# Second attention of a two-layer attention and mixture-of-experts kernel: order of context and X loads, shared root steps, and earlier routing steps

## The reference, cut to what matters

```
B, S, D, KEYS, E = 16, 112, 256, 375, 8
x = x + xattn0(layernorm(x), ctx)          # 16 heads, projections
x = x + ffn0(layernorm(x))                 # top-2 of 8 experts, gelu, per-expert capacity
# second layer: what the change touches
q = layernorm(x)
e = (q @ ctx.T) / sqrt(D)                  # per batch, 112 x 375
e = e - (1 - mask[b, s]) * 1e9
x = x + softmax(e) @ ctx                   # per batch, 112 x 256
# second ffn
logits = layernorm(x) @ gate_w             # 112 x 8 per batch
mult, sel = sparse_mixer(logits)           # top 2 of 8, two gates per token
x = x + sum over chosen experts of w * (silu(x w1) * (x w3)) w2
```

## Time and profile before

| | |
|---|---|
| median of three runs | 1080.9 us (1079.68 to 1085.33) |
| the profiled execution: its time, its span | 1085.0 us, 1083.1 us |
| PE, DVE, ACT, POOL busy | 949.7, 685.8, 544.7, 478.4 us |
| mean granted clock of PE | 0.937 |
| DMA | 160.1 MB, mean 148 GB/s |
| last layer-0 row in PSUM read by DVE; first hidden matmul of layer 1 | 615.29 us; 755.64 us |

### The profile page before, as it was taken

One profiled execution on the slowest core, in us unless ns is written; L12 is line 12 of the kernel. 1 busy time (PEld: TensorE's weight loads), 2 busy tenths in 40 slices (PEclk: granted clock), 3 DMA queues, 4 the chain that ended last, 5 costly groups with the idle time before them and its releaser, 6 DMA issues.

```text
span 1083.1 us, 23135 instructions
## 1 busy us (share of the span) xinstructions
PE 949.7 (88%) x8011; PEld 872.0 (81%) x8011; DVE 685.8 (63%) x1937; ACT 544.7 (50%) x1212; POOL 478.4 (44%) x478
## 2 busy tenths in 40 slices
PE   4889999999999568999999758772999999999997
PEld 4778888778877468998999735562999999999997
DVE  6456676676666666666666435674667788777242
ACT  3678888878888545455555313321323433433120
POOL 2022235225223346666666523376355455545323
PEclk9799999999999779999999969875999999999999
DMA  7878888977774268667766685544353445433101
GB/s 187 166 211 186 201 196 214 247 182 188 188 169 108 60 184 209 152 160 160 182 165 163 150 208 163 163 134 151 118 141 93 106 113 153 113 100 81 20 3 23
DMA packets 109671, 160.10 MB, mean 148 GB/s; under 512 B 11361, under 2 KB 98625, under 8 KB 107617
## 3 DMA queue, kind: packets, MB, share of 16 engines
q1 hardware_dynamic: 95600, 140.03, 49.3%
q0 software_dynamic: 13936, 18.33, 8.7%
HBM read 103.32 MB, written 56.96 MB: 148 GB/s over the span
## 4 chain that ended last, share of the span: by engine, by line
PE 43%; DVE 8%; POOL 5%; issue 4%; DMA 4%; ACT 1%; POOLq 0%; SPq 0%; DVEq 0%; ACTq 0%
PE ps L300 37%; DVE HTH L1293 2%; POOL x_scratch L1545 2%; PE ps L647 1%; PE ps L490 1%; DMA CN<-in_ctx_n 1%; PE ps L578 1%; POOL xg_scratch L1481 1%; DMA x_scratch<-YY,XG 1%; POOL rs L1460 1%; DVE WL L915 1%; PE ps L595 1%; POOL HTL L1533 1%; DVE st L1113 1%; DMA XG<-xg_scratch 1%
## 5 line engine op out<-in xcount | busy, mean ns | idle before, releaser
L300 PE MATMUL ps<-XGH,WH 128*128 128x280 f32 (+1 forms) x768 | 224.9, 293 | 9.6 <-ACT GT L816 7.4
L300 PE MATMUL ps<-XGL,WH 128*128 128x280 f32 (+1 forms) x768 | 224.1, 292 | 0.0
L300 PE MATMUL ps<-XGH,WL 128*128 128x280 f32 (+1 forms) x768 | 223.9, 292 | 0.0
L1533 POOL TENSOR_TENSOR HTL<-GT,HTH 128x280 fp32r<-128x280 f32 x128 | 132.6, 1049 | 168.3 <-DVE HTH L1293 168.3
L1165 DVE CUSTOM_DVE_ANT_0 NS<-ps,negm 112x375 f32<-112x375 f32 x256 | 138.0, 545 | 91.2 <-PE ps L406 90.1
L300 PE MATMUL ps<-WH,HTH 128*112 128x256 f32 x568 | 162.1, 285 | 1.5 <-DVE YY L1307 1.5
L300 PEld LDWEIGHTS ps<-XGH,WH 128*128 128x128 f32 x768 | 148.9, 194 | 14.4 <-ACT GT L816 10.8
L300 PE MATMUL ps<-WL,HTH 128*112 128x256 f32 x568 | 159.6, 281 | 0.0
L300 PE MATMUL ps<-WH,HTL 128*112 128x256 f32 x568 | 159.5, 281 | 0.0
L744 ACT ACTIVATE PP<-NS,MN 112x375 f32<-112x375 f32 x256 | 156.8, 613 | 3.4 <-DVE MN L1165 2.9
L300 PEld LDWEIGHTS ps<-XGH,WL 128*128 128x128 f32 x768 | 149.1, 194 | 0.0
(11 more groups left out here) (206 smaller groups left out, 1893.4 us busy)
## 6 DMA issues: line engine op xcount, KB each, us to landing
WG<-in_v SPq DMA_DIRECT2D x48, 512.0 KB, 4.1
KST<-k_scratch SPq DMA_DIRECT2D x48, 376.0 KB, 5.5
WG<-in_w SPq DMA_DIRECT2D x32, 512.0 KB, 4.5
k_scratch<-KHL SPq DMA_DIRECT2D x64, 188.0 KB
CT<-in_ctx_t SPq DMA_DIRECT2D x32, 375.0 KB, 7.4
xg_scratch<-zero SPq DMA_DIRECT2D x8, 1289.8 KB, 10.3
xg_scratch<-zero SPq DMA_DIRECT2D x16, 586.2 KB, 9.0
XG<-xg_scratch SPq DMA_DIRECT2D x14, 586.2 KB, 4.6
```

The costliest lines, as they stand in the source:

```text
L300: m = e.matmul(out_ap, l, r, start=n == 0, stop=n == len(steps) - 1)
L1533: e.tensor_tensor(HTL[:, f, cols], GT[:, gi % 3, :], HTH[:, f, cols], ALU.subtract).then_inc(hl_pool[layer], 1)
```

## The change

- `CHUNKS1` becomes 3, 3, 3, 3, 2, 2.
- CT2 and CN are moved in memory behind the tile XG of layer 0, over the tiles that the hidden and the row matmuls read, so they can be loaded once those matmuls are done.
- In the last expert of layer 0, ACT, DVE and POOL handle chunks 38 and 39 before the row blocks (DVE: chunk 38 before the first).
- SP issues CT2(0) and CT2(1) before the last two weight chunks (after the last hidden matmul), CN(0) after the last row matmul, and only then waits for the row adds. After them: X 0 to 1, X 2 to 3, CT2(2), CN(1), X 4 to 7, CT2(3), CN(2), X 8 to 15, CN(3), then CT2(4) and so on, CT2(b) with CN(b-4) from b = 8.
- POOL waits for both statistics of a step and does both roots with one addition and one power.
- DVE's stage order becomes `attended`, `inverse`, `mins`, `normed4`, `normed3`, `stats3`; up to three routing instructions are placed behind each and six at the end of a step, the older group first. A group's lists begin at the end of step 11, counts and exponential come in step 13, DVE's part behind them right after `attended` of that step (after `normed4` in the last step).
- POOL's scatter of batch b comes at step 12 + nb + b while the step is below 23, the rest after the last root.

```
+                last = layer == 0 and ex == E - 1          # ACT, POOL; DVE alike, inside the row loop
+                for c in range(per - 2 if last else 0):
+                    lo(base + per * ex + 10 + c)
...
+            for t in range(B + 9):
+                for stage, fn in ((8, attended), (6, inverse), (4, mins), (9, normed4), (1, normed3), (0, stats3)):
                     if 0 <= t - stage < B:
                         fn(t - stage)
+                        if stage == (8 if t < B + 8 else 9) and t >= 13:
+                            counted(t - 13)
+                        advance_pairs(routes, 3)
+                if t >= 11:
+                    route(t - 11)
+                advance_pairs(routes, 6 if t < B else 12)
...
+            def roots(t):
+                new, old = t - 1 < B, t - 9 >= 0
+                if new:
+                    e.wait_ge(var3, t)
+                if old:
+                    e.wait_ge(var4, t - 8)
+                i = (t - 1) % 2
+                cols = slice(4 + i if new else 6 + i, 7 + i if old else 5 + i, 2)
+                if t > 2:
+                    e.wait_ge(rs34, t - 2)
+                e.tensor_scalar(rs[:, cols], st2[:, cols, 1], EPS, None, ALU.add).then_inc(eps, 1)
...
+                e.tensor_tensor(rs[:, cols], rs[:, cols], half, ALU.pow).then_inc(rs34, 1)
...
+            for t in range(1, B + 9):
+                roots(t)
                 for b0, nb in CHUNKS1:
+                    if 0 <= t - 12 - b0 - nb < nb and t < B + 7:
+                        pool_scatter(e, 1, sent)
+                        sent += 1
+            for b in range(sent, B):
+                pool_scatter(e, 1, b)
...
+                if layer == 0 and ex == E - 1:
+                    e.wait_ge(h_mm[0], 16 * E)
+                    context_t(e, 0)
+                    context_t(e, 1)
...
+            e.wait_ge(y_mm[0], 5 * E)
+            context_n(0)
+            for n in range(5 * E - NY, 5 * E):
+                e.wait_ge(*row_done(0, n))
             kept(0)
+            kept(1)
+            context_t(e, 2)
+            context_n(1)
+            kept(2)
+            context_t(e, 3)
+            context_n(2)
+            kept(3)
+            context_n(3)
+            for b in range(4, B + 4):
+                if b < B:
+                    context_t(e, b)
+                if b - 4 >= 4:
+                    context_n(b - 4)
```

More of the change, by code:

```diff
@@ L846, in act_experts @@
                     n = base + per * ex + 10 + c
-                    if c < per - 2 and n < NCHUNK:
+                    if c < per - 2 and n < NCHUNK and not last:
                         act_weights_hi(e, n)
@@ L890, in gate_exp, with gate_after @@
                 e.activation(v, v, ACT.Exp, scale=-1.0).then_inc(r_exp, 1)
[L892 to L895, removed]
+            def gate_after(b):
+                if ends_chunk1(b) is not None:
+                    gate_exp(ends_chunk1(b))
+            for t in range(B + 13):
+                for stage, fn in ((11, logits_out), (13, gate_after), (10, x4_out), (6, copies), (5, exps), (2, x3_out)):
                     if 0 <= t - stage < B:
@@ L1084, in build_kernel, with __init__, step @@
         class Route:
-            def __init__(self, steps):
-                self.steps, self.at = steps, 0
+            def __init__(self, steps, order=(0, 0)):
+                self.steps, self.at, self.order = steps, 0, order
+            def step(self, routes):
+                Chain.at = self.at
+                got = next(self.steps, "end")
+                self.at, Chain.at = Chain.at, Chain.n
+                if got == "end":
+                    routes.remove(self)
+                return got not in ("end", "blocked")
         placed = set()
@@ L1095, in advance @@
                 for r in list(routes):
[L1096 to L1101, removed]
+                    if r.step(routes):
                         if in_turn:
@@ L1105, in advance, with advance_pairs @@
                         break
+        def advance_pairs(routes, n):
+            taken = 0
+            for i in range(n):
+                for r in sorted(routes, key=lambda r: (r.order[0], (r.order[1] + i) % 2)):
+                    if r.step(routes):
+                        taken += 1
+                        break
+            return taken
         def dve_flags(e, layer):
@@ L1327, in dve_experts @@
                             lo(n)
+                last = layer == 0 and ex == E - 1
                 for c in range(5):
@@ L1561, in pool_experts @@
                             lo(n)
+                last = layer == 0 and ex == E - 1
+                for c in range(per - 2 if last else 0):
+                    lo(base + per * ex + 10 + c)
                 for c in range(5):
                     rows_added(ex, c)
-                    if c < per - 2:
+                    if c < per - 2 and not last:
                         lo(base + per * ex + 10 + c)
@@ L1785, in sp_attention1 @@
         def sp_attention1(e):
-            for n in range(5 * E - NY, 5 * E):
-                e.wait_ge(*row_done(0, n))
             def kept(i):
```

100 lines of the change are left out of this document (51 added, 49 removed).

## The result

The changed kernel takes 1078.97 us (median of 20 runs, 1069.23 to 1087.74), the kernel before 1083.03 beside it on the same chip (20 runs, 1077.05 to 1090.71). The ratio is 0.9957, with an interval of 0.9936 to 0.9977: 4 us faster, just inside the 0.5% that one measurement can tell. The forecast was 1069.7 and its range ended at 1076, so both are missed. It started from a median of 1080.9 for the kernel before, which over 20 runs is 1083.03; so 2.1 us of the miss are the base, and the rest is the gain, 4 us for 11.2. What came is near the size of rival C: only the tail gains.

What follows compares the result with a forecast made beforehand. Second attention was taken as bound by a hole, a 4.70 us loop, routing and a scatter tail, with CN's DMA engines close behind. Gains 5.4 + 0.8 + 5.0 = 11.2 us from 1080.9 gave 1069.7, range 1059 to 1076.

Steps and rivals of the forecast that it cites:

- rival C: Second attention: early loads only displace X, the queue decides, only the tail gains 5 us: 1076; chance 0.13.
- 5: DMA engines carrying CN: CN(15) lands at 710.5 to 711; batch 15 taken as attended at 714, 5.4 us sooner.
- step 3: Start of second attention: no wait for CN(0), batch 0 6.3 us sooner; PE then stands 5 to 6 us for CT2(4).
- the third: The 5 of 16 DMA engines said to carry each 125-partition CN load, 3.26 us apiece, and never to rest.
- Step 1: Chunks 38 and 39 before the rows: the last row add goes at about 617.0, a gain of 0.5 us.
- Step 2: Early CT2(0), CT2(1) and CN(0) fill the queue: X 0 to 1 lands at about 627, a loss of 3 us.
- Step 4: Attention loop, shared root and new DVE order: steps of 3.6 to 4.4 us, plus 3.4, put batch 15 at 714.5.
- Step 6: Routing counts at step 13, bank freed behind `attended`: PE's 3.71 us stand and the slow matmuls after it go.
- Step 7: Tail: 16 scatters behind the last root instead of 20, 5.0 us less; the last root follows batch 15 0.8 sooner.
- B: Second attention: DMA has room and the loop runs at PE's pace, batch 15 at 704: 1059.7; chance 0.20.
- D: POOL in order: shared root held behind scatters waiting for destinations, up to 3 us a step, slower: 1090.3; chance 0.07.
- A: The forecast itself: 5 us of the gain in the stage, 6 behind it, range 1064 to 1074; chance 0.60.

Runs made afterwards that it cites:

- the scatter run: Changed kernel with the scatters placed three steps later, 20 behind the last root instead of 16; ratio 0.9996 to the kernel before.
- second and third group: Follow-up runs, against the kernel before at 1109.1 and 1110.7 us; every profile shows a lower granted clock, 0.915 to 0.928.
- first and fourth group: Follow-up runs, against the kernel before at 1082.3 and 1082.5 us; granted clock 0.936 to 0.940 and 0.928 to 0.943.

## Why the prediction was wrong

**The step that failed is 5**, with 3, which it was to confirm: "CN(15) lands at 710.5 to 711, so batch 15 is attended at 712 to 713", because the third "never rests" and starts with two CT2 and one CN done. It did rest, and PE's wait for CT2(4), put at 5 to 6 us in step 3, was 8.78 and 9.60. Windows of 2 us (busy PE, PEld, DVE, ACT, POOL, clock, DMA share, GB/s), and SP's issues:

```profile
650.00:652.00 2.00, 0.00 (x0) 0.00 (x0) 0.00 (x0) 0.00 (x0) 0.00 (x0) 0.50 0.47 131
652.00:654.00 2.00, 1.77 (x3) 1.07 (x4) 0.00 (x0) 0.00 (x0) 0.00 (x0) 0.50 0.32 116
654.00:656.00 2.00, 2.00 (x6) 1.22 (x5) 0.92 (x4) 0.36 (x1) 0.00 (x0) 0.50 0.05 19
```

```profile
634.87 4.14 SPq L1866 DMA_DIRECT2D CN<-in_ctx_n  x1
639.05 16.39 SPq L1808 DMA_DIRECT2D CT<-in_ctx_t  x5
655.49 0.38 SPq L1866 DMA_DIRECT2D CN<-in_ctx_n  x1
659.05 0.38 SPq L1808 DMA_DIRECT2D CT<-in_ctx_t  x1
659.47 0.36 SPq L1866 DMA_DIRECT2D CN<-in_ctx_n  x1
```

Four buffers hold CT2. CT2(8) can be issued only when `scores` of batch 4 have run, and those stood 8.78 us for CT2(4). CN(4) is behind CT2(8) in SP's order, so it goes at 655.49, into engines whose share has fallen to 0.05. Most of the head start of 7 us of loads is used up at that moment. My own arithmetic with the right start gives: eight pairs at 4.6, four CN at 3.26 and three stores at 2.3 are 56.7, from 655.5 that is 712.2, against 713.5 in the kernel before. The value matmuls of batches 12, 13 and 14 wait, and batch 15's follow at 713.81; with the CN load cut these waits are gone, so it is CN that they wait for:

```profile
701.52 1.52 PE L597 MATMUL ps<-CN,PT 125*112 125x256 f32 x6 [1.25 <-issue]
...
704.98 1.52 PE L597 MATMUL ps<-CN,PT 125*112 125x256 f32 x6 [1.07 <-issue]
...
710.12 1.66 PE L597 MATMUL ps<-CN,PT 125*112 125x256 f32 x6 [1.70 <-issue]
```

Batch 15 is attended at 717.25 for the 714 forecast. Of these 3.25 us the later start explains about 1.5 (712.2 for 710.5 to 711). The rest is argued and not shown: batch 15's value matmuls begin 1.6 us behind that sum and run at a granted clock of 0.50. In the second profile batch 15 is at 119.8 instead of 116.5 behind the last hidden matmul, for which I have no cause. Point by point:

- **Step 1**, last row add at 617.0, gain 0.5: wrong, 620.18, a loss of 2.7. I looked at ACT's gate and not at the buffer of the row copy. The row add issued at 609.54 took 8.81 us, and the fifth copy needs its buffer. The queue is too full for it: the zeros are in it in the kernel before too, where no copy waits, but on top of them either the moved chunks or the early loads are enough to make a copy wait. With the zeros moved away, both together are not. Step 2 named this ("row adds slowed too") only as its worst case of 5 us.
- **Step 2**, X 0 to 1 at 627: right by size (628.07), wrong in its way. X came late since the last row add did, and in 624 to 628 the DMA engines were half idle:

```profile
616.00:620.00 4.00, 0.00 (x0) 0.00 (x0) 0.42 (x1) 0.51 (x1) 0.30 (x1) 0.90 1.14 280
...
624.00:628.00 4.00, 0.00 (x0) 0.00 (x0) 0.00 (x0) 0.00 (x0) 0.00 (x0) 0.50 0.47 130
```

- **Step 3**: batch 0 at 642.5, measured 643.66. The wait for CT2(4) was put at 5 to 6 us and is 8.78, batch 1 at 655.5 and is at 657.48. The mechanism is right and its size 3 us short.
- **Step 4**, 59.0 us from batch 1 to batch 15: measured 59.8 and 62.1. With CN cut and nothing else it is 59.1, so the sum of steps is right for a loop that no load holds, in part by luck: the first four steps take 14.2 us for 15.8, the last four 18.7 for some 16. From batch 8 to 15 all six profiles of changed kernels with the cut show 30.9 or 31.0, those of the changed kernel 31.7 and 32.7: that is the third again.
- **Step 6**: PE's stand of 3.71 us for the bank is gone, as forecast.
- **Step 7**: 2.12 us to the root and 16 scatters, as forecast; 4.5 us in place of 5.0. None of the scatters was to wait; one waits 1.41 us for destinations, and from the last scatter on it goes 0.4 us faster. The cover held: destinations of the last group 12.0 us behind the root.

In sum 5.4, 0.8 and 5.0 were forecast; on average over two profiles each -0.7, 0.75 and 4.5 came.

**The rivals.** C is what happened: X comes 4 us later (27.3 for 23.2), by the early loads or by the moved chunks, each of which is enough, and the queue holds the stage. B did not come: DMA has room only with CN cut, and then batch 15 is at 107.2 and the time 1070.0, where B had 103.3 and 1059.7. D's mechanism is there at the size of my step 4: the scatter run moves batch 15 by 3 to 6 us where 3.4 stood in the sum. It was wrong to let A and B hold 0.80 of the chance after finding a bound that the whole stage must pass: A rested on a head start of 7 us of loads being kept, and nothing in the trace said it would be.

**What was not tried**: more than four buffers for CT2, CN or the row copies, so whether the head start could be kept is open, and that the four buffers are what loses it is read from the trace and not shown by a run. What makes the stage differ by 2 to 3 us between two profiles of the same kernel is open as well.

## What to carry to other kernels

Before crediting loads with a head start, follow them to the moment at which their ring is full and the queue waits for the consumer again: what the consumer loses there the queue can lose too. A mean DMA share of 0.5 can be a bound; find a stretch in which one kind of load moves alone, take its share and rate, and count how long that part of the engines is busy over the stage. Where two bounds lie close, test each removed alone and both together: here the changes of the computation alone gave 0.25% (0 to 0.5%), the cut alone nothing, both 1.3%; the versions with both, with or without CT2(4) ahead (0.984 to 0.987), are the best, and the runs do not tell them apart.

## What the runs showed of the hardware that I had not expected

- The first row add of the last expert took 8.81 us, with the DMA engines at a share of 1.07 to 1.14; the last one took 4.97, against 3.46 for the last one of before.
- In all eight profiles of the second and third group DVE's short routing instructions behind the last root stand between one another while POOL issues scatters, 4 to 11 us together. The scatter run has it worst (DVE, then POOL's wait for the destinations):

```profile
749.78 0.26 DVE L1065 SCALAR_TENSOR_TENSOR r_w<-r_x,mx 112x16 f32<-112x16 f32 x2 [0.49 <-DVE r_sel L935]
...
753.28 0.35 DVE L951 RECIPROCAL r_w<-r_w 112x32 f32<-112x32 f32 x1 [1.94 <-remote]
...
754.69 0.18 DVE L935 TENSOR_TENSOR r_sel<-r_sel,tq 112x16 f32<-112x16 f32 x1 [1.06 <-DVE r_w L951]
```

```profile
760.27 0.94 POOL L1524 DMA_INDIRECT xg_scratch<-XN,dest  x1 [6.49 <-issue]
```

  None of the profiles of the first and fourth group has it. There the last destinations of the changed kernel come 12.0 us behind the root, here 16.8 to 25.1, and POOL waits 3.1 to 6.5 us. So the cover of step 7 fails in some groups of runs, and part of the scatter run's loss (6.49 us of its tail) is this and not the four scatters. The kernel before was profiled only where it does not show; what causes it is open.
